# Half-angle features in place of the octant form, spread over thirteen steps

## The chip, the cores and the metric

One Trainium2 chip, one of its cores. The metric is the device time of the whole kernel in microseconds; lower is better. Engines: TensorE (PE, weight loads PEld), VectorE (DVE), ScalarE (ACT), GpSimd (POOL), SyncE (SP).

## The reference

Three chunked self-attention layers (8 heads, chunks of 64, followed by a residual and a layer norm) and one neighbour layer, on 32 batches of 128 x 1024. The change lies in the neighbour layer. It takes for each of 1024 points of three coordinates the 30 nearest, and from each difference three features:

```python
idx = _knn(x_loc, k)
rel = pts[bidx, idx] - pts[:, :, None, :]
xr, yr, zr = (rel[..., 0], rel[..., 1], rel[..., 2])
sxy2 = xr * xr + yr * yr
r2 = sxy2 + zr * zr
rho = jnp.sqrt(jnp.maximum(r2, TINY))
sxy = jnp.sqrt(jnp.maximum(sxy2, TINY))
theta = jnp.arctan2(jnp.where(deg_r, 0.0, zr), jnp.where(deg_r, 1.0, sxy))
phi = jnp.arctan2(jnp.where(deg_p, 0.0, yr), jnp.where(deg_p, 1.0, xr))
feat = jnp.concatenate([sph, sph - jnp.mean(sph, axis=-1, keepdims=True)], axis=-1)
h = lrelu(_bn(feat @ W1.T, g1, b1))
...
att = jax.nn.softmax(h[..., 0], axis=-1)
agg = jnp.einsum('bnkc,bnk->bnc', xk, att)
```

Here deg_r and deg_p are r2 < TINY and sxy2 < TINY, and sph is the three features.

## The kernel before

Three stages stand behind one another. attention_and_neighbours does the attention layers, the neighbour search and the features; batch_norms reads the features back and makes the attention weights of the neighbours; neighbour_sum adds them up. A barrier ends each stage. The change touches the first stage and one line of the second.

The first stage walks through 32 batches in steps. A batch has 24 steps (3 layers x 8 pairs of chunks); a loop body holds two batches, 48 steps. All engines run the same step function, each with its own part, in order, and semaphores tie them together. In each step TensorE makes the scores of one pair (SC, two buffers), VectorE takes their row_max (L1065), ScalarE makes the exponentials (L724, eight with a read of the sum), VectorE inverts the sum one step later (row_rec, L1073), GpSimd multiplies (L845), TensorE transposes three steps later, ScalarE copies that out (prob_t, L731), and so on. The scores of step s need the exponentials of step s - 2. Between these stand the projections and their copies (q_t, k_t, v_b), and VectorE's search for the 32 nearest (MAX8, FIND_INDEX8, MATCH_REPLACE8).

Work on a finished batch lags behind: the function lagging(i, s, at) gives the batch whose work with lag `at` belongs into step s, counted from the first step of that batch's attention plus 24. The lag numbers are the order written out by hand. In lags 8 to 33 the neighbours' coordinates are fetched tile by tile (hot L1104 on VectorE, fetch on TensorE, picked L750 on ScalarE, select on GpSimd, every third step). Then come the features of 256 x 128 differences, as tiles of 128 x 256 per quantity:

- lag 34 GpSimd: apart, the difference (L941). Lag 35 ScalarE: sqr, its squares (L761).
- lag 36 GpSimd: r2, two sums (L947, L949); r2m, its maximum with TINY (L952); good, its test against TINY (L953).
- lag 38 ScalarE: root (L767). Lag 39 and 40 GpSimd: degen (L959), yy (L960), xx (L962, L966, L970).
- lag 41 ScalarE: Abs of yy and xx (L771, L772). Lag 42 ScalarE: signs (L777, L778, L780); VectorE: big, the larger (L1109), and its reciprocal (L1112).
- lag 43 VectorE: the smaller (L1115) and a flag (L1116). Lag 44 ScalarE: turn, quarter (L784, L785), arctangent (L790); GpSimd: ratio (L975).
- lag 45 to 47 GpSimd: angle times turn, plus quarter, the half turn, the sign (L980 to L996). Lag 47 SyncE: three stores.

Root and arctangent need other tables of ScalarE than the exponential: a table load stands before each, and one before the next exponential. After the last batch, TAIL = 48 further steps finish the lagging work.

## Time and profile before

| | |
|---|---|
| median of 3 runs | 6427.92 us (6425.65 to 6432.02) |
| profiled execution | 6420.67 us, span 6418.8 us |
| first stage | to about 4741 us of the span |
| granted TensorE clock, mean | 0.919 |
| touched instructions before | GpSimd 15, ScalarE 10, VectorE 4 for each batch |

Times are microseconds from the start of the span. Busy times of neighbouring instructions on one engine overlap slightly, so start to start is the better measure of what one costs its engine. In brackets stands the idle time of the engine before an instruction and what ended it.

### The profile page before, as it was taken

To read this page: it belongs to the slowest core of one execution; us is meant where nothing else is said; L and a number is where in the kernel's file an instruction comes from. 1 tells how busy PE (TensorE), PEld (TensorE's weight loads), DVE (VectorE), ACT (ScalarE), POOL (GpSimd) and SP (SyncE) were. 2 spreads that over 40 slices of the span, in tenths; PEclk is the share of its full clock that TensorE was granted. 3 is DMA by queue.
4 is the path that set the end of the run, shared out by engine and by line. 5 is a ranking of instruction groups with operands and counts; after the bars stand their busy time and mean duration, and the time that the engine had idled before them with its cause. 6 is when DMAs were issued, how large, how long until landed. Compare 5 with 4: busy or idle time off the path is not lost. (4 is left out here: it accounts for less than half of the span.)

```text
span 6418.8 us, 227467 instructions
## 1 busy us (share of the span) xinstructions
PE 5554.2 (87%) x82516; PEld 3410.8 (53%) x82516; DVE 5771.8 (90%) x8140; ACT 4559.4 (71%) x17241; POOL 3506.7 (55%) x3471
## 2 busy tenths in 40 slices
PE   7988888889888888888888888888759949999999
PEld 3555555555555555455555555455423337777776
DVE  7999999999999999999999999999946687777776
ACT  7888888888888888888888888888713633333333
POOL 3466666666666666666666666666640023333332
PEclk9999999989999999999999999999869979999999
DMA  2333333333333333233333333333340023333332
GB/s 44 94 105 93 98 96 95 90 95 104 100 103 96 97 96 96 88 95 98 105 101 99 96 96 97 89 95 101 97 122 0 0 59 84 86 92 91 86 90 75
DMA packets 651349, 568.72 MB, mean 89 GB/s; under 512 B 553072, under 2 KB 574832, under 8 KB 616208
## 3 DMA queue, kind: packets, MB, share of 16 engines
q1 hardware_dynamic: 613264, 284.51, 18.9%
q10 hardware_dynamic: 36864, 268.45, 11.6%
q8 instruction: 702, 11.50, 0.7%
q14 instruction: 519, 4.25, 0.2%
HBM read 384.76 MB, written 67.24 MB: 70 GB/s over the span
## 5 line engine op out<-in xcount | busy, mean ns | idle before, releaser
L724 ACT ACTIVATE prob<-SC,row_max 128x64 f32<-128x64 f32 x6144 | 1841.8, 337 | 423.5 <-DVE row_max L1065 415.5
L845 POOL TENSOR_TENSOR prob<-prob,row_rec 128x512 f32<-128x512 f32 x768 | 800.6, 1042 | 1413.3 <-DVE row_rec L1073 1405.0
L724 ACT ACTIVATION_READ_ACCUMULATOR prob<-SC,row_max 128x1 f32 x6144 | 1393.1, 229 | 0.0
L1057 DVE FIND_INDEX8 nbr<-top,dist 128x8 uint16<-128x1024 f32 x1024 | 1236.2, 1220 | 0.0
L1050 DVE MAX8 top<-dist 128x8 f32<-128x1024 f32 x1024 | 1192.1, 1206 | 1.6
L1052 DVE MATCH_REPLACE8 dist<-top,dist 128x1024 f32<-128x1024 f32 x768 | 925.4, 1210 | 0.0
L588 PE MATMUL SC<-k_bd,q_t 128*64 128x256 f32 x6144 | 906.3, 419 | 0.0
L609 PE MATMUL PT<-ident,prob 128*128 128x128 f32 x3072 | 503.9, 289 | 463.6 <-ACT prob_t L731 462.8
L609 PEld LDWEIGHTS PT<-ident,prob 128*128 128x128 f32 x3072 | 374.5, 148 | 941.6 <-issue 909.9
L1721 ACT ACTIVATE dense<-DM 128x512 f32<-128x512 f32 x512 | 305.6, 597 | 745.6 <-PE DM L1680 745.0
L1829 DVE TENSOR_TENSOR d_oh_a<-lo,iota_a 128x4096 bf16<-128x4096 bf16 x256 | 583.8, 2291 | 237.8 <-PE DM L1680 237.3
L560 PEld LDWEIGHTS G<-table,low_all 128*128 128x128 bf16 x24576 | 672.3, 97 | 189.3 <-issue 112.2
L560 PE MATMUL G<-table,low_all 128*128 128x24 bf16 x24576 | 708.6, 175 | 58.5 <-DVE low_all L1104 33.1
L1680 PEld LDWEIGHTS DM<-placed,d_oh_a 128*128 128x128 bf16 x24576 | 646.5, 96 | 110.8 <-issue 77.7
L1680 PE MATMUL DM<-placed,d_oh_a 128*128 128x32 bf16 x24576 | 652.0, 177 | 30.8 <-DMA placed<-compact 22.5
L1065 DVE TENSOR_REDUCE row_max<-SC 128x8 f32<-128x512 f32 x768 | 522.0, 680 | 96.5 <-PE SC L588 96.2
L588 PEld LDWEIGHTS SC<-k_bd,q_t 128*64 128x64 f32 x6144 | 396.0, 144 | 321.3 <-issue 222.3
L602 PE MATMUL PD<-ctx 128*128 128x512 f32 x1024 | 544.3, 613 | 0.0
L731 ACT ACTIVATE prob_t<-PT 128x512 f32<-128x512 f32 x768 | 498.4, 649 | 0.6 <-PE PT L609 0.6
L1658 PE MATMUL AG<-dense,x_t 128*128 128x512 f32 x1024 | 474.4, 606 | 1.1 <-issue 0.7
L717 ACT ACTIVATE dist<-PD,xcol 128x512 f32<-128x512 f32 x512 | 369.6, 722 | 135.3 <-PE PD L602 118.9
L538 PE MATMUL PJ<-ctx,w_in 128*128 128x512 f32 x768 | 439.0, 654 | 0.1
(195 smaller groups left out, 9805.5 us busy)
## 6 DMA issues: line engine op xcount, KB each, us to landing
low_all<-low_scratch ACTq DMA_DIRECT2D x256, 1024.0 KB, 5.1
k_bd<-k_t SPq DMA_DIRECT2D x3072, 16.0 KB, 1.9
placed<-compact SPq DMA_DIRECT2D x256, 192.0 KB, 3.9
ctx<-in_ctx SPq DMA_DIRECT2D x32, 512.0 KB, 4.0
mask<-in_mask SPq DMA_DIRECT2D x32, 512.0 KB, 6.7
xb<-in_x SPq DMA_DIRECT2D x32, 512.0 KB, 3.4
x_scratch<-xb SPq DMA_DIRECT2D x32, 512.0 KB, 4.7
y_scratch<-y_b SPq DMA_DIRECT2D x32, 512.0 KB, 4.7
```

The costliest lines, as they stand in the source:

```text
L560: last = pe.matmul(G[:, g * 24:(g + 1) * 24], hot[:, t % 2, col:col + 128], table[:, v % BPB, part, :], start=(part == 0), stop=(part == 2))
L588: last = pe.matmul(bank[64 * ch:64 * ch + 64, cols], q_t[:, w % 2, here], k_bd[:, s // 2 % KEY_BUFS, s % 2 * 2 + ch, cols], start=False, s ...
L602: pe.matmul(PD[:, :], ctx[:, u, t * 128:(t + 1) * 128], ctx[:, u, h * HALF:(h + 1) * HALF], start=False, stop=True).then_inc(pd_ready, 1)
L609: last = pe.transpose(PT[:, m * 128:(m + 1) * 128], prob[:, r % 4, m * 128:(m + 1) * 128], ident[:, :])
L724: last = act.activation(prob[:, s % 4, g * CHUNK:(g + 1) * CHUNK], SC[:, s % 2, g * CHUNK:(g + 1) * CHUNK], ACT.Exp, bias=row_max[:, s % 2 ...
L845: pool.tensor_tensor(pr, pr, row_rec[:, r % 2, :].unsqueeze(2).to_broadcast([128, 8, CHUNK]), ALU.mult).then_inc(normed, 1)
L1050: dve.max(best, row).then_inc(top_step, 1)
L1052: dve.match_replace(row, best, row, NEG_BIG).then_inc(top_step, 1)
L1057: last = dve.max_index(nbr[:, uu % BPB, t, k * 8:(k + 1) * 8], best, row)
L1065: dve.tensor_reduce(row_max[:, s % 2, :], SC[:, s % 2, :].rearrange("p (h k) -> p h k", h=8), AX.X, ALU.max, negate=True).then_inc(maxed, 1)
L1680: last = pe.matmul(DM[:, x % DM_BANKS, (g % 16) * 32:(g % 16 + 1) * 32].rearrange("p (q m) -> p q m", q=4), oh_a[:, t % 2, g, :], placed[: ...
L1829: dve.tensor_tensor(oh_a[:, t % 2, :, :].rearrange("p g (a two) -> p g a two", two=2), lo2[:, u, t, :, :].unsqueeze(2).to_broadcast(wide), ...
```

## The change

The arctangents are taken of half the angle: tan(a / 2) = y / (hypotenuse + |x|). That needs no comparison of |x| and |y|, no smaller and larger, no quarter turn. The root is taken of three quantities instead of two (r2m gets a third column, made by a third sum on GpSimd), `sides` holds them and |across|. `base` is the sum of two neighbouring sides on GpSimd, inverted on VectorE at lag 43; `ratio` is legs times that. Abs and signs are of half the width and all stand at lag 41 on ScalarE. `turn` on GpSimd at lag 45 gives the half turn of the second angle, and two half-width operations at lag 46 end the work. The stores stay at lag 47. The two tensor_scalar of lag 36 get a second operation, times 1.0. The missing factor 2 goes into two columns of the next stage's weights.

```diff
@@ -47,14 +47,15 @@
 LINKS = 7
-TABLE_LINKS, SELECT_LINKS, TURN_LINKS = 4, 3, 4
+TABLE_LINKS, SELECT_LINKS, R2_LINKS = 4, 3, 3
 
 HOT_AT, FETCH_AT, SELECT_AT = 8, 10, 12
-APART_AT, R2_AT, YX_AT, ABS_AT, RATIO_AT, ANGLE_AT, TURN_AT, SPH_AT = 34, 36, 39, 41, 42, 44, 46, 47
-TAIL = SPH_AT + 1
+APART_AT, SQUARE_REL_AT, R2_AT, ROOT_AT, LEGS_AT, ACROSS_AT, BASE_AT, INVERSE_AT = 34, 35, 36, 38, 39, 41, 42, 43
+RATIO_AT, ANGLE_AT, TURN_AT, SPH_AT, SPH_OUT_AT = 44, 44, 45, 46, 47
+TAIL = SPH_OUT_AT + 1
 GROUPS = 32
@@ -222,16 +223,14 @@
         r2 = sb("r2", [128, 2, NF])
-        r2m = sb("r2m", [128, 2, NF])
-        root = sb("root", [128, 2, NF])
+        r2m = sb("r2m", [128, 3, NF])
+        sides = sb("sides", [128, 4, NF])
         good = sb("good", [128, 2, NF])
-        degen = sb("degen", [128, 2, NF])
-        yy = sb("yy", [128, 2, NF])
-        xx = sb("xx", [128, 2, NF])
-        big, ratio = sqr[:, 0:2, :], apart[:, 0:2, :]
+        legs = sb("legs", [128, 2, NF])
+        signs = sb("signs", [128, 2, NF])
         angle = sb("angle", [128, 2, NF])
-        hot, ay, ax, flag, sph = low_all, r2, r2m, r2, angle
-        turn, quarter, down_sign, left_sign, left_half = good, degen, yy, xx[:, 1, :], xx[:, 0, :]
+        hot, ratio, base = low_all, apart[:, 0:2, :], sqr[:, 0:2, :]
+        across, turn, left_half = r2[:, 0, :], r2[:, 1, :], good[:, 0, :]
 
...
@@ -496,15 +495,14 @@
                             sp.dma_start(own[32 * q:32 * q + 32, c, :, :], mine[row, q:q + 1].broadcast_to([32, NT, GROUPS])).then_inc(own_in, 16)
-                v = lagging(i, s, SPH_AT)
+                v = lagging(i, s, SPH_OUT_AT)
                 if v is not None:
                     b = i * BPB + v
-                    sp.wait_ge(root_ready, START + b + 1)
                     sp.wait_ge(sph_ready, START + b + 1)
                     alone(sp)
-                    sp.dma_start(dram["sph"][0][b], root[:, 0, :]).then_inc(sph_out, 16)
+                    sp.dma_start(dram["sph"][0][b], sides[:, 0, :]).then_inc(sph_out, 16)
                     for c in range(2):
-                        sp.dma_start(dram["sph"][1 + c][b], sph[:, c, :]).then_inc(sph_out, 16)
+                        sp.dma_start(dram["sph"][1 + c][b], angle[:, c, :]).then_inc(sph_out, 16)
 
@@ -755,34 +753,26 @@
                     load_low(i, at[0], at[1] + 2)
-                v = lagging(i, s, APART_AT + 1)
+                v = lagging(i, s, SQUARE_REL_AT)
                 if v is not None:
                     act.activation(sqr[:, :, :], apart[:, :, :], ACT.Square).then_inc(sqr_ready, 1)
-                v = lagging(i, s, R2_AT + 2)
+                v = lagging(i, s, ROOT_AT)
                 if v is not None:
                     b = i * BPB + v
-                    act.wait_ge(good_ready, START + b + 1)
+                    act.wait_ge(r2_ready, START + b + 1)
                     act.wait_ge(sph_out, START + b * 48)
-                    act.activation(root[:, :, :], r2m[:, :, :], ACT.Sqrt).then_inc(root_ready, 1)
-                v = lagging(i, s, ABS_AT)
-                if v is not None:
-                    act.wait_ge(yx_ready, START + i * BPB + v + 1)
-                    act.activation(ay[:, :, :], yy[:, :, :], ACT.Abs)
-                    act.activation(ax[:, :, :], xx[:, :, :], ACT.Abs).then_inc(abs_ready, 1)
-                v = lagging(i, s, ABS_AT + 1)
+                    act.activation(sides[:, 0:3, :], r2m[:, :, :], ACT.Sqrt).then_inc(sides_ready, 1)
+                v = lagging(i, s, ACROSS_AT)
                 if v is not None:
                     b = i * BPB + v
-                    act.wait_ge(abs_ready, START + b + 1)
-                    act.activation(down_sign[:, :, :], yy[:, :, :], ACT.Sign, scale=SIGN_SCALE, bias=turns[:, 0:1])
-                    act.activation(left_sign[:, :], xx[:, 1, :], ACT.Sign, scale=SIGN_SCALE, bias=turns[:, 0:1]).then_inc(signs_ready, 1)
-                    act.wait_ge(signs_ready, START + b + 1)
-                    act.activation(left_half[:, :], left_sign[:, :], ACT.Identity, scale=-float(np.pi / 2), bias=turns[:, 1:2])
-                v = lagging(i, s, RATIO_AT + 2)
-                if v is not None:
-                    act.wait_ge(least_ready, START + i * BPB + v + 1)
-                    act.activation(turn[:, :, :], flag[:, :, :], ACT.Identity, scale=-2.0, bias=1.0)
-                    act.activation(quarter[:, :, :], flag[:, :, :], ACT.Identity, scale=float(np.pi / 2))
+                    act.wait_ge(legs_ready, START + b + 1)
+                    act.wait_ge(sph_out, START + b * 48)
+                    act.activation(sides[:, 3, :], across, ACT.Abs).then_inc(across_ready, 1)
+                    act.activation(signs[:, 0, :], across, ACT.Sign, scale=SIGN_SCALE, bias=turns[:, 0:1]).then_inc(sign_step, 1)
+                    act.activation(signs[:, 1, :], legs[:, 1, :], ACT.Sign, scale=SIGN_SCALE, bias=turns[:, 0:1])
+                    act.wait_ge(sign_step, START + b + 1)
+                    act.activation(left_half, signs[:, 0, :], ACT.Identity, scale=-float(np.pi / 4), bias=turns[:, 1:2]).then_inc(signs_ready, 1)
                 v = lagging(i, s, ANGLE_AT)
@@ -843,6 +833,12 @@
                     pool.tensor_tensor(pr, pr, row_rec[:, r % 2, :].unsqueeze(2).to_broadcast([128, 8, CHUNK]), ALU.mult).then_inc(normed, 1)
+                v = lagging(i, s, BASE_AT)
+                if v is not None:
+                    b = i * BPB + v
+                    pool.wait_ge(sides_ready, START + b + 1)
+                    pool.wait_ge(across_ready, START + b + 1)
+                    pool.tensor_tensor(base[:, :, :], sides[:, 1:3, :], sides[:, 2:4, :], ALU.add).then_inc(base_ready, 1)
                 part = s % BSTEPS - SPLIT_AT
@@ -945,55 +941,40 @@
                     pool.tensor_tensor(r2[:, 1, :], sqr[:, 0, :], sqr[:, 2, :], ALU.add).then_inc(r2_step, 1)
-                    pool.wait_ge(r2_step, START + b + 1)
-                    pool.tensor_tensor(r2[:, 0, :], r2[:, 1, :], sqr[:, 1, :], ALU.add).then_inc(r2_ready, 1)
-                    pool.wait_ge(r2_ready, START + b + 1)
+                    pool.wait_ge(r2_step, START + b * R2_LINKS + 1)
+                    pool.tensor_tensor(r2[:, 0, :], r2[:, 1, :], sqr[:, 1, :], ALU.add).then_inc(r2_step, 1)
+                    pool.wait_ge(r2_step, START + b * R2_LINKS + 2)
                     alone(pool)
-                    pool.tensor_scalar(r2m[:, :, :], r2[:, :, :], TINY, None, ALU.max)
-                    pool.tensor_scalar(good[:, :, :], r2[:, :, :], TINY, None, ALU.is_ge).then_inc(good_ready, 1)
-                v = lagging(i, s, YX_AT)
+                    pool.tensor_scalar(r2m[:, 0:3:2, :], r2[:, :, :], TINY, 1.0, ALU.max, ALU.mult).then_inc(r2_step, 1)
+                    pool.tensor_scalar(good[:, :, :], r2[:, :, :], TINY, 1.0, ALU.is_ge, ALU.mult).then_inc(good_ready, 1)
+                    pool.wait_ge(r2_step, START + b * R2_LINKS + 3)
+                    pool.tensor_tensor(r2m[:, 1, :], r2m[:, 2, :], sqr[:, 1, :], ALU.add).then_inc(r2_ready, 1)
+                v = lagging(i, s, LEGS_AT)
                 if v is not None:
                     pool.wait_ge(good_ready, START + b + 1)
+                    pool.wait_ge(r2_ready, START + b + 1)
                     alone(pool)
-                    pool.tensor_scalar(degen[:, :, :], good[:, :, :], -1.0, 1.0, ALU.mult, ALU.add).then_inc(degen_ready, 1)
-                    pool.tensor_tensor(yy[:, :, :], apart[:, 1:3, :], good[:, :, :], ALU.mult)
-                    pool.wait_ge(root_ready, START + b + 1)
-                    pool.tensor_tensor(xx[:, 0, :], root[:, 1, :], good[:, 0, :], ALU.mult)
-                v = lagging(i, s, YX_AT + 1)
+                    pool.tensor_tensor(across, apart[:, 0, :], good[:, 1, :], ALU.mult)
+                    pool.tensor_tensor(legs[:, :, :], apart[:, 1:3, :], good[:, :, :], ALU.mult).then_inc(legs_ready, 1)
+                v = lagging(i, s, TURN_AT)
                 if v is not None:
                     b = i * BPB + v
-                    pool.tensor_tensor(xx[:, 1, :], apart[:, 0, :], good[:, 1, :], ALU.mult).then_inc(yx_step, 1)
-                    pool.wait_ge(yx_step, START + b + 1)
-                    pool.wait_ge(degen_ready, START + b + 1)
-                    alone(pool)
-                    pool.tensor_tensor(xx[:, :, :], xx[:, :, :], degen[:, :, :], ALU.add).then_inc(yx_ready, 1)
-                v = lagging(i, s, ANGLE_AT)
+                    pool.wait_ge(signs_ready, START + b + 1)
+                    pool.tensor_tensor(turn, left_half, signs[:, 1, :], ALU.mult).then_inc(turn_ready, 1)
+                v = lagging(i, s, RATIO_AT)
                 if v is not None:
                     b = i * BPB + v
-                    pool.wait_ge(least_ready, START + b + 1)
-                    pool.tensor_tensor(ratio[:, :, :], ratio[:, :, :], big[:, :, :], ALU.mult).then_inc(ratio_ready, 1)
-                v = lagging(i, s, ANGLE_AT + 1)
+                    pool.wait_ge(inverse_ready, START + b + 1)
+                    pool.tensor_tensor(ratio[:, :, :], legs[:, :, :], base[:, :, :], ALU.mult).then_inc(ratio_ready, 1)
+                v = lagging(i, s, SPH_AT)
                 if v is not None:
                     pool.wait_ge(angle_ready, START + b + 1)
-                    pool.tensor_tensor(angle[:, :, :], angle[:, :, :], turn[:, :, :], ALU.mult).then_inc(turn_step, 1)
-                v = lagging(i, s, TURN_AT)
-                if v is not None:
-                    b = i * BPB + v
-                    pool.wait_ge(turn_step, START + b * TURN_LINKS + 1)
-                    alone(pool)
-                    pool.tensor_tensor(angle[:, :, :], angle[:, :, :], quarter[:, :, :], ALU.add).then_inc(turn_step, 1)
-                    pool.wait_ge(turn_step, START + b * TURN_LINKS + 2)
-                    pool.tensor_tensor(angle[:, 1, :], angle[:, 1, :], left_sign[:, :], ALU.mult).then_inc(turn_step, 1)
-                    pool.wait_ge(turn_step, START + b * TURN_LINKS + 3)
-                    pool.tensor_tensor(angle[:, 1, :], angle[:, 1, :], left_half[:, :], ALU.add).then_inc(turn_step, 1)
-                v = lagging(i, s, SPH_AT)
-                if v is not None:
-                    b = i * BPB + v
-                    pool.wait_ge(turn_step, START + b * TURN_LINKS + 4)
-                    alone(pool)
-                    pool.tensor_tensor(sph[:, :, :], angle[:, :, :], down_sign[:, :, :], ALU.mult).then_inc(sph_ready, 1)
+                    pool.wait_ge(turn_ready, START + b + 1)
+                    pool.tensor_tensor(angle[:, 1, :], angle[:, 1, :], signs[:, 0, :], ALU.mult).then_inc(flip_step, 1)
+                    pool.wait_ge(flip_step, START + b + 1)
+                    pool.tensor_tensor(angle[:, 1, :], angle[:, 1, :], turn, ALU.add).then_inc(sph_ready, 1)
 
@@ -1102,18 +1083,11 @@
                     dve.tensor_scalar(hot[:, t % 2, :], low_all[:, t % 2, :], iota_p[:, 0:1], None, ALU.is_equal).then_inc(hot_ready, 1)
-                v = lagging(i, s, RATIO_AT)
+                v = lagging(i, s, INVERSE_AT)
                 if v is not None:
                     b = i * BPB + v
-                    dve.wait_ge(abs_ready, START + b + 1)
-                    dve.tensor_tensor(big[:, :, :], ax[:, :, :], ay[:, :, :], ALU.max).then_inc(big_step, 1)
-                    dve.wait_ge(big_step, START + b + 1)
-                    alone(dve)
-                    dve.reciprocal(big[:, :, :], big[:, :, :])
-                v = lagging(i, s, RATIO_AT + 1)
-                if v is not None:
-                    dve.tensor_tensor(ratio[:, :, :], ax[:, :, :], ay[:, :, :], ALU.min)
-                    dve.tensor_tensor(flag[:, :, :], ay[:, :, :], ax[:, :, :], ALU.is_gt).then_inc(least_ready, 1)
+                    dve.wait_ge(base_ready, START + b + 1)
+                    dve.reciprocal(base[:, :, :], base[:, :, :]).then_inc(inverse_ready, 1)
 
@@ -1392,6 +1367,7 @@
             link(dve.scalar_tensor_tensor(v1[:, :, :], w1s[:, :].unsqueeze(2).to_broadcast([128, 6, 3]), -1.0 / 3.0, v1[:, :, :], ALU.mult, ALU.add))
+            link(dve.tensor_scalar(v1[:, :, 1:3], v1[:, :, 1:3], HALF_ANGLES, None, ALU.mult))
 
@@ -1941,7 +1917,7 @@
     out["pow_half"] = np.full((128, 1), -0.5, np.float32)
-    out["turns"] = np.tile(np.array([SIGN_TIE, np.pi / 2], np.float32), (128, 1))
+    out["turns"] = np.tile(np.array([SIGN_TIE, np.pi / 4], np.float32), (128, 1))
     out["iota8"] = high_bits(np.tile(np.arange(8, dtype=np.float32)[None, :], (128, 1)))
```

## Rows read from the trace of the kernel before

**Rows 1.** The page, part 1: busy us (share of the span) and instructions
```profile
PE 5554.2 (87%) x82516; PEld 3410.8 (53%) x82516; DVE 5771.8 (90%) x8140; ACT 4559.4 (71%) x17241; POOL 3506.7 (55%) x3471
```

**Rows 2.** Windows from:to: length, busy us of PE PEld DVE ACT POOL, PEclk, DMA
```profile
1000.00:4000.00 3000.00, 2627.53 (x36246) 1563.56 (x36243) 2926.67 (x4505) 2587.56 (x10644) 1975.67 (x2056) 0.92 0.34 97
...
4620.00:4741.00 121.00, 36.47 (x1116) 32.46 (x1116) 48.53 (x49) 32.30 (x56) 89.41 (x89) 0.53 0.32 111
```

**Rows 3.** Waits: who waited for whom, us in total, times, longest us
```profile
DVE row_max L1065 <- PE SC L588: 96.2, 59, 14.0
```

**Rows 4.** Timeline of VectorE, lags 42 and 43: start us, us, instruction
```profile
2132.29 1.46 DVE L1109 TENSOR_TENSOR sqr<-r2m,r 128x512 f32<-128x512 f32 x1
...
2133.90 3.35 DVE L1112 RECIPROCAL sqr<-sqr 128x512 f32<-128x512 f32 x1
...
2141.36 0.68 DVE L1115 TENSOR_TENSOR apart<-r2m,r 128x512 f32<-128x512 f32 x1
...
2142.56 0.69 DVE L1065 TENSOR_REDUCE row_max<-SC 128x8 f32<-128x512 f32 x1
```

**Rows 5.** Timeline of ScalarE, lag 44
```profile
2146.71 0.70 ACT L784 ACTIVATE good<-r 128x512 f32<-128x512 f32 x1
...
2147.93 1.28 ACT L790 ACT_TABLE_LOAD   x1
```

**Rows 6.** Timeline of TensorE, lags 44 and 46, with idle time before in brackets
```profile
2140.95 1.09 PE L609 MATMUL PT<-ident,prob 128*128 128x128 f32 x4 [5.47 <-ACT prob_t L731]
...
2156.01 0.76 PE L609 MATMUL PT<-ident,prob 128*128 128x128 f32 x4 [2.27 <-ACT prob_t L731]
```

**Rows 7.** Window of TensorE's scores for lag 47
```profile
2158.00:2162.00 4.00, 4.00 (x57) 2.77 (x56) 2.07 (x6) 3.38 (x19) 3.77 (x6) 0.50 0.09 37
```

**Rows 8.** Timeline of VectorE: first, middle and last of 30 waits at lag 47
```profile
422.71 0.69 DVE L1065 TENSOR_REDUCE row_max<-SC 128x8 f32<-128x512 f32 x1 [1.44 <-PE SC L588]
...
2161.23 0.69 DVE L1065 TENSOR_REDUCE row_max<-SC 128x8 f32<-128x512 f32 x1 [1.93 <-PE SC L588]
...
4615.11 0.69 DVE L1065 TENSOR_REDUCE row_max<-SC 128x8 f32<-128x512 f32 x1 [1.81 <-PE SC L588]
```

**Rows 9.** Groups of ScalarE, root and Square: busy us, mean ns, idle before
```profile
L767 ACT ACTIVATE root<-r2m 128x512 f32<-128x512 f32 x32 | 20.2, 631 | 7.6 <-POOL good L953 7.3
...
L761 ACT ACTIVATE sqr<-apart 128x768 f32<-128x768 f32 x32 | 29.0, 906 | 6.0 <-POOL apart L941 6.0
```

**Rows 10.** Timeline of TensorE at lag 40 and of VectorE into lag 41
```profile
2110.31 0.37 PE L583 MATMUL SC<-mask_row,two_chunks 64*128 64x512 bf16 x1 [1.90 <-ACT v_b L677]
...
2118.74 1.21 DVE L1052 MATCH_REPLACE8 dist<-top,dist 128x1024 f32<-128x1024 f32 x1
...
2119.95 0.69 DVE L1065 TENSOR_REDUCE row_max<-SC 128x8 f32<-128x512 f32 x1
```

**Rows 11.** Groups of GpSimd: busy us, mean ns of one, idle before
```profile
L952 POOL TENSOR_SCALAR r2m<-r 128x512 f32<-128x512 f32 x32 | 49.2, 1537 | 6.2 <-POOL r L949 6.2
...
L959 POOL TENSOR_SCALAR degen<-good 128x512 f32<-128x512 f32 x32 | 19.8, 619 | 0.3 <-POOL good L953 0.2
...
L970 POOL TENSOR_TENSOR xx<-xx,degen 128x512 f32<-128x512 f32 x32 | 40.8, 1274 | 6.5 <-POOL xx L966 6.5
...
L966 POOL TENSOR_TENSOR xx<-apart,good 128x256 f32<-128x256 f32 x32 | 23.4, 732 | 0.0
```

**Rows 12.** Timeline of GpSimd, last batch, first and last instruction of its features
```profile
4710.24 1.80 POOL L941 TENSOR_TENSOR apart<-rel,own 128x768 f32<-128x768 f32 x1
...
4736.73 1.26 POOL L996 TENSOR_TENSOR angle<-angle,yy 128x512 f32<-128x512 f32 x1 [0.18 <-POOL angle L990]
```

**Rows 13.** Timeline of ScalarE, root of the last batch but one
```profile
4665.04 0.63 ACT L767 ACTIVATE root<-r2m 128x512 f32<-128x512 f32 x1 [3.84 <-POOL good L953]
```

**Rows 14.** Timeline of ScalarE and GpSimd at lag 42
```profile
2127.69 0.31 ACT L724 ACTIVATE prob<-SC,row_max 128x64 f32<-128x64 f32 x1 [0.35 <-DVE row_max L1065]
...
2128.15 1.03 POOL L845 TENSOR_TENSOR prob<-prob,row_rec 128x512 f32<-128x512 f32 x1
```

17 lines of the change are left out of this document (9 added, 8 removed).

## Prediction

> **What bounds the kernel now.** I read the busy line of the page first: VectorE 90%, TensorE 87%, ScalarE 71%, GpSimd 55% [rows 1]. An average over stages doesn't name a bound, so the windows came next [rows 2]. From 1000 to 4000 us VectorE is busy 2926.67 of 3000 us (97.6%), ScalarE 86%, GpSimd 66%. From 4620 to 4741 us no engine is full, GpSimd leads with 89.41 of 121 us, and the granted clock of TensorE is 0.53, near its lower level of 1.2 GHz. So the first stage has a steady part that VectorE paces, and a tail that is a chain. The waits then say where VectorE's missing 2.4% goes: into row_max waiting for TensorE's scores, 96.2 us in all [rows 3].
>
> The touched work runs once for each of 32 batches: 30 times in the steady part, twice in the tail. I name steps by lag: "lag 42" is RATIO_AT of before.
>
> **VectorE, steady part.** Removed are max (L1109), min (L1115) and is_gt (L1116). The reciprocal stays and moves from lag 42 to 43. Busy times overlap the next instruction, so I take start to start [rows 4]: L1109 to L1112 2133.90 - 2132.29 = 1.61 us; L1115 to the row_max of the next step 2142.56 - 2141.36 = 1.20 us. Together 2.81 us a batch, all of it on the engine that paces and none of it waiting. L1109 is stretched (1.46 us busy, where the like-shaped min has 0.68); without that the gain would be 0.78 less. I take the record: 30 x 2.81 = 84.3 us. The moved reciprocal (3.35 us) makes lag 42 some 5.0 us shorter and lag 43 2.1 us longer. Its result goes to `ratio` on GpSimd at lag 44, which is queued behind a normalisation that needs a row_rec that VectorE issues after the reciprocal, so nobody waits longer for it. ScalarE is no limit there: it waits for row_max in both steps.
>
> **ScalarE.** Ten activations become seven. The switches to root and arctangent and back stay, so no table load is saved. What counts is lag 44, where `turn` and `quarter` stood ahead of the arctangent: 2147.93 - 2146.71 = 1.22 us [rows 5]. Queued behind it are copies, the reload of the exponential's table, the exponentials and prob_t. TensorE then waits 2.27 us for that prob_t [rows 6] and goes on at a granted clock of 0.50, 1.2 GHz [rows 7]; VectorE waits 1.93 us for the scores that follow [rows 8]. This happens at lag 47 in all 30 steady batches, first at 422.71 and last at 4615.11 us, 54.1 us in sum, 0.38 (two of them) to 2.34 us each [rows 8]. ScalarE 1.22 us earlier takes as much from 28 waits and all of two: 28 x 1.22 + 2 x 0.38 = 34.9 us. Bounds: 0 (TensorE late for a reason of its own) and 54.1 (its clock stays at 2.4 GHz). I take 34.9, because TensorE will reach that prob_t earlier than now and still idle some 2 us before it. The activations gone at lag 41 and 42 are worth nothing, since ScalarE then waits for VectorE; lag 41 itself gets four half-width operations for two full ones, some 0.5 us more, in that spare time.
>
> The root goes from 512 to 768 columns: 631 ns, against 906 for the Square of 768 [rows 9], 0.27 us more. It has no cover. TensorE waits 1.90 us at lag 40 for a v_b copy queued behind the root, and at lag 41 row_max starts 1.21 us after the operation before it, the whole busy time, without the usual overlap of 0.08 [rows 10]: this chain is just late. 30 x 0.27 = 8.2 us lost; bounds 0 and 15 (if TensorE's slow clock also lasts longer).
>
> **GpSimd.** Fifteen instructions, 15.7 us, become twelve. A two-input one takes 1274 ns for 512 columns and 732 for 256, a tensor_scalar with two operations 619 (L959) [rows 11]. New sum: seven half-width ones 5.1, three full ones (legs, base, ratio) 3.85, r2m and good 1.24: 10.2 us. The 5.5 us less are worth nothing in the steady part, where GpSimd mostly waits for row_rec. `base` at lag 42 now stands ahead of the row split and the selection of a tile, for which ScalarE's copy of the next tile waits. By adding up the queue the selection ends about when ScalarE comes: nothing, at most 1 us a batch if ScalarE has no spare time there. Sharing of memory access with VectorE shifts both ways; I keep 10 us either way.
>
> The neutral second operation (max, then times 1) is to bring r2m and good from 1537 ns down to 619 [rows 11]. L952 has one operation, L959 two; but L959 is mult and add, so the rows leave open whether the count or the kind decides. I take the count. The price is 1.8 us for each of two batches in the tail, nothing in the steady part.
> The Trainium skill (GPSIMD Engine Reference, "3.1 Elementwise — side-by-side cycle accounting") has a body of up to two operations bound by its port at 1.03 cycles an element, which makes the two forms equal and the edit worthless. L952 against L959 speaks against the rule here; by it the sum would be the third rival's.
>
> **The tail.** The last batch's features run from `apart` at 4710.24 to the end of L996 at 4738.0 us, 27.8 us with nothing beside them [rows 12]. Out of that chain go, at the durations of rows 4 and 11: degen 0.62, one half-width product 0.72, xx plus degen and its fence 1.46, max and its fence 0.84, min and is_gt 1.20, the tensor_scalar saving 1.75, angle times turn and plus quarter 2.78, the last product 1.44, the narrower Abs 0.3, and 1.15 of table load, since a root here starts right at the end of a wait for GpSimd, its load done within it [rows 13]. Into it: third column 0.73, base 1.27. 12.26 - 2.00 = 10.3 us. Before that, features of the last batch but one hold up the last one's tiles; I give this GpSimd's 5.5 us and 1.5 us of waits for Abs and min: 7 us, bounds 0 and 15. Tail: 17.3 us. Doubling two weight columns in the next stage costs some 0.2 us once.
>
> **Sum.** 84.3 + 34.9 - 8.2 + 17.3 - 0.2 = 128.1 us. The profiled execution took 6420.67 us (span 6418.8), which gives 6292.6; it lies 7.25 us under the median of 6427.92. Comparisons go by medians, so the forecast is 6427.92 - 128.1 = 6300 us. Nothing else changes behind 4741 us.
>
> **Rivals.** First: TensorE's clock stays up from lag 45 on and those waits vanish. For it: the idle time of 5.47 us at lag 44 [rows 6] nearly goes. Against: it still idles for prob_t. 19.2 us more: 6281 us.
> Second: the saving is given back. If the scores come at a pace set by ScalarE and TensorE, VectorE arrives earlier and waits. For it: the late row_max at lag 41 and 47. Against: before 2140.95 TensorE idles 5.47 us, so it is ahead where VectorE gains. Price: half of 84.3 and all of 34.9: 6300 + 42 + 35 = 6377 us.
> Third: the neutral operation does nothing, all else holds: 3.5 us more in the tail, 6303 us.
> Fourth, slower: GpSimd's wait for `across` at lag 42, ahead of split, selection and the next normalisation. ScalarE is through lag 41 before 2127.69, when its 0.35 us wait ends, so `across` is there by 2127.8; GpSimd gets to the wait at 2128.15 + 1.03 = 2129.2 [rows 14]. 1.4 us are spare; past that each microsecond delays tile copy and exponentials. The sum turns at 128 / 30 = 4.3 us more, 5.7 us late; at 6.5 us late it is 6300 + 30 x 5.1 = 6453 us. Nothing in the record has ScalarE that late.
>
> **Chances.** Forecast 0.57, rivals 0.15, 0.13, 0.11 and 0.02, the remaining 0.02 within 0.2%, which is 13 us and about what a measurement of this kernel tells from no change. Faster 0.95, same 0.02, slower 0.03 (the fourth and a hundredth for the unseen). Range: the low end adds to the first rival a tail of 25 us and part of the some 23 us of waits outside lag 47 and the first steps: 6260. The high end has VectorE's 84.3 with 10 us of contention against it and a tail of 7: 6347.
>
> **What would show it.** L1109, L1115, L1116 gone and L1112 still 3.35 us; the pitch of the batches down from (4615.11 - 422.71) / 29 = 144.6 us to about 140.9; row_max's wait at lag 47 near 0.65 us instead of 1.8; at lag 41 a new wait of 0.2 to 0.3; r2m and good at 0.62 us (third rival: 1.5); the stage ending near 4613 instead of 4741 us. The forecast is wrong if row_max's waits don't shrink, if ScalarE or GpSimd waits for base, across or the selection, or if the reciprocal runs longer in its new place.

## The result: 6319.5 us, and the profile after

The kernel with the change took 6319.46 us (median of 4 runs, 6316.55 to 6323.72), beside it the kernel before 6429.97 us (4 runs, 6425.65 to 6432.29). The ratio is 0.9829, with a 95% interval of 0.9812 to 0.9846: faster by 110.5 us, where 128.1 were forecast. The profiled execution has a span of 6314.8 us, against 6418.8.

First the page of the kernel after, part 1, which answers to [rows 1]:

```profile
PE 5517.6 (87%) x82516; PEld 3384.3 (54%) x82516; DVE 5699.2 (90%) x8045; ACT 4499.4 (71%) x17145; POOL 3397.5 (54%) x3375
```

VectorE's busy time fell by 72.6 us, not by 84.3. The windows of the same kernel (length, busy us of PE, PEld, DVE, ACT, POOL, granted clock, DMA share, GB/s):

```profile
1000.00:4000.00 3000.00, 2655.17 (x36940) 1576.22 (x36937) 2940.94 (x4536) 2603.24 (x10807) 1938.98 (x2030) 0.94 0.35 99
4513.00:4634.00 121.00, 46.60 (x1281) 39.15 (x1281) 53.62 (x62) 39.03 (x103) 92.82 (x96) 0.55 0.34 120
```

VectorE is now busy 98.0% of the steady part instead of 97.6% [rows 2]: it is the bound as before, and even more so. The last 121 us of the stage are still a chain of GpSimd at a low granted clock. Where the time went is read from the groups (line, engine, operation, tiles, count | busy us, mean ns of one | idle before):

```profile
L1046 DVE TENSOR_REDUCE row_max<-SC 128x8 f32<-128x512 f32 x768 | 518.6, 675 | 73.7 <-PE SC L586 73.3
L1085 DVE TENSOR_SCALAR low_all<-low_all,iota_p 128x4096 bf16<-128x4096 bf16 x256 | 364.1, 1422 | 34.5 <-DMA low_all<-low_scratch 34.5
...
L1090 DVE RECIPROCAL sqr<-sqr 128x512 f32<-128x512 f32 x32 | 106.8, 3338 | 22.4 <-POOL sqr L841 22.4
...
L835 POOL TENSOR_TENSOR prob<-prob,row_rec 128x512 f32<-128x512 f32 x768 | 830.2, 1082 | 1433.5 <-DVE row_rec L1054 1403.5 <-issue 30.0
...
L948 POOL TENSOR_SCALAR r2m<-r 128x512 f32<-128x512 f32 x32 | 62.0, 1936 | 6.2 <-POOL r L945 6.2
L949 POOL TENSOR_SCALAR good<-r 128x512 f32<-128x512 f32 x32 | 61.8, 1932 | 2.5
```

Four things stand there. The wait of row_max for scores went from 96.2 [rows 3] to 73.3 us. `r2m` takes 1936 ns, not 619 and not 1537 [rows 11]. L1085, a line the change doesn't touch, got longer: this compare (it turns a tile's low indices into a one-hot matrix, 256 of them) took 347.1 us before, 1356 ns each, and takes 364.1 now, 1422 ns. And the multiplication on `prob` on GpSimd, 1042 ns before, takes 1082. The compares also explain the first number: the three removed instructions took 2.79 us a batch on the mean from start to start, 89.3 us in 32 batches, and 89.3 less 17.0 is 72.3.

The timeline of VectorE of the kernel after, first and last wait at lag 47, which answer to [rows 8]:

```profile
418.69 0.69 DVE L1046 TENSOR_REDUCE row_max<-SC 128x8 f32<-128x512 f32 x1 [1.45 <-PE SC L586]
...
4520.94 0.69 DVE L1046 TENSOR_REDUCE row_max<-SC 128x8 f32<-128x512 f32 x1 [1.26 <-PE SC L586]
```

(4520.94 - 418.69) / 29 = 141.46 us a batch, against 144.56: 3.10 us less, 3.70 forecast. All 30 waits are still there, 33.8 us in sum instead of 54.1. From the last of them to the end of the stage, which is the minus_half memset at 4634.12 us (4741.40 before), 113.2 us pass instead of 126.3: the tail gives 13.1 us.

From here on "pitch" is the mean distance of the reciprocals of batches 1 to 30, L1090 or its like (before 144.57, after 141.48, so 3.10 less before rounding), and "waits" are those of row_max for scores behind the first of them (before 76.5 us, after 54.2).

### The profile page after: what moved, and what is told of

Read it like the earlier page. It is cut to its first block and busy times, and to the rows that moved or that the text cites. A ratio compares the mean times of both kernels' runs of the same rounds, so it can differ in the third digit from the quotient of the medians.

```text
span 6314.8 us, 227176 instructions
## 1 busy us (share of the span) xinstructions
PE 5517.6 (87%) x82516; PEld 3384.3 (54%) x82516; DVE 5699.2 (90%) x8045; ACT 4499.4 (71%) x17145; POOL 3397.5 (54%) x3375
## 5 line engine op out<-in xcount | busy, mean ns | idle before, releaser
L835 POOL TENSOR_TENSOR prob<-prob,row_rec 128x512 f32<-128x512 f32 x768 | 830.2, 1082 | 1433.5 <-DVE row_rec L1054 1403.5
L607 PEld LDWEIGHTS PT<-ident,prob 128*128 128x128 f32 x3072 | 361.7, 145 | 833.8 <-issue 815.6
L607 PE MATMUL PT<-ident,prob 128*128 128x128 f32 x3072 | 490.9, 284 | 351.0 <-ACT prob_t L729 350.3
L1046 DVE TENSOR_REDUCE row_max<-SC 128x8 f32<-128x512 f32 x768 | 518.6, 675 | 73.7 <-PE SC L586 73.3
```

The costliest lines, as they stand in the source:

```text
L607: last = pe.transpose(PT[:, m * 128:(m + 1) * 128], prob[:, r % 4, m * 128:(m + 1) * 128], ident[:, :])
L835: pool.tensor_tensor(pr, pr, row_rec[:, r % 2, :].unsqueeze(2).to_broadcast([128, 8, CHUNK]), ALU.mult).then_inc(normed, 1)
```

## The experiments

Three theories were tried, each against the others. A: ScalarE's load at lag 44 sets the wait at lag 47. B: the kind of operation, not its count, sets what GpSimd's tensor_scalar costs. C, formed from the compare above: GpSimd's timing decides how long VectorE's compares take. All ratios are against the kernel before, measured beside each run; its median was 6431.34 us beside the first four, 6430.24 beside the next four and 6426.98 beside the last two. The kernel of the change did not run beside them, so a difference to its 6319.46 us can be off by some 4 us from that alone. Medians are of four executions, except ten for the neutral operations on the kernel before and two for the narrow root.

### Neutral second operations taken away

```diff
-pool.tensor_scalar(r2m[:, 0:3:2, :], r2[:, :, :], TINY, 1.0, ALU.max, ALU.mult).then_inc(r2_step, 1)
-pool.tensor_scalar(good[:, :, :], r2[:, :, :], TINY, 1.0, ALU.is_ge, ALU.mult).then_inc(good_ready, 1)
+pool.tensor_scalar(r2m[:, 0:3:2, :], r2[:, :, :], TINY, None, ALU.max).then_inc(r2_step, 1)
+pool.tensor_scalar(good[:, :, :], r2[:, :, :], TINY, None, ALU.is_ge).then_inc(good_ready, 1)
```

> The changed kernel, the two tensor_scalar of lag 36 with one operation again. Theory A (the second operation lengthens r2m and good from 1.5 to 1.94 us, GpSimd gets late, its normalisation at lag 38 falls on VectorE's compare and stretches it from 1.28 to 1.83 us): both at 1.50, the compare of lag 38 back to 1.28, pitch of the batches 141.5 down to 141.0 to 141.2 us, time 6319 less 10 to 17 us. Rival B (GpSimd's length is covered in the steady part, as the prediction had it): same pitch, only the tail 1 to 2 us shorter, 6317 us. Rival C (the second operation pays): slower by 1.8 us in each of two tail batches.

Measured: 6316.82 us (6310.49 to 6318.49), ratio 0.982 (0.9802 to 0.9837), pitch 141.53. `r2m` and `good` take 1508 and 1497 ns. The second operation costs 0.43 us each time and buys nothing, and in the steady part it costs no time. From the last lag-47 wait (4524.32) to the end of the stage (4634.64) it is 110.3 us, 2.9 less than with the second operations.

Rival B holds for the time, and theory A failed at its main point: the compare at lag 38 stayed long in every batch from 400 to 4500 us, 1.76 us on the mean instead of the expected 1.28. From the timeline of this run, lag 38:

```profile
1503.10 1.05 POOL L835 TENSOR_TENSOR prob<-prob,row_rec 128x512 f32<-128x512 f32 x1
...
1503.47 1.77 DVE L1085 TENSOR_SCALAR low_all<-low_all,iota_p 128x4096 bf16<-128x4096 bf16 x1
```

With the shorter `r2m` and `good` the addition on `y_b` is done in time, but the multiplication on `prob` behind it now starts 0.37 us ahead of the compare. In the same batch of the kernel before it starts 1.06 us ahead (1526.23, compare at 1527.29) and ends just in time. The difference, 0.69 us, is about the third column's addition, 0.73 us, which stands in GpSimd's chain here and not before. So that addition is enough to make the compare late. It was not taken out by itself.

### VectorE's three operations put back

They work on tiles that are there (max into `r2m` at lag 42, min into `apart` and is_gt into a spare tile at lag 43); what they compute is used by nobody.

```diff
+                v = lagging(i, s, BASE_AT)
+                if v is not None:
+                    dve.wait_ge(base_ready, START + i * BPB + v + 1)
+                    dve.tensor_tensor(r2m[:, 0:2, :], legs[:, :, :], legs[:, :, :], ALU.max)
 ...
+                    dve.tensor_tensor(apart[:, 0:2, :], legs[:, :, :], legs[:, :, :], ALU.min)
+                    dve.tensor_tensor(spare[:, :, :], legs[:, :, :], legs[:, :, :], ALU.is_gt)
-                    dve.wait_ge(base_ready, START + b + 1)
                     dve.reciprocal(base[:, :, :], base[:, :, :]).then_inc(inverse_ready, 1)
```

> The changed kernel with three two-input VectorE operations of the removed length put back (one at lag 42, two at lag 43), results unused. Theory A (VectorE paces, each is paid in full): pitch up by 0.60 + 0.60 for two and 0.6 to 1.6 for the first, 1.8 to 2.8 us a batch, time 6319 + 58 to 90 us, the waits at lag 47 unchanged at 0.4 to 1.45 us. Rival B (the saving was partly given back in waits): pitch up by less than 1.4 us, 45 us in all, and the waits at lag 47 get shorter.

Measured: 6399.49 us (6392.86 to 6401.77), ratio 0.9953 (0.9935 to 0.997), pitch 143.73, 2.25 more than after. Its row of the waits (total us, times, longest):

```profile
DVE row_max L1047 <- PE SC L587: 57.5, 48, 13.6
```

The three put back take 2.90 us a batch here, start to start (0.59, 0.87 and 1.44 by the trace; those of the kernel before took 1.59, 0.60 and 0.60). The pitch shows 2.25 of it. The rest is mostly paid out of waits (73.3 after, in the count of this row): behind the first reciprocal they fall from 54.2 to 38.7 us, 0.53 a batch. 2.25 + 0.53 = 2.78, against the forecast's 2.81. So the pitch and time are theory A's, and the shorter waits at lag 47 are rival B's.

The waits at lag 47 alone are 14.3 us here, in 16 of 30 batches. Against the 54.1 of before, 39.8 are gone without VectorE's gain, where the forecast had 34.9; the reciprocal stands one step later than before in this run too, so not all of it need be ScalarE's. With VectorE's gain on top, 33.8 us are left: 19.5 of the 39.8 come back as waits.

### ScalarE's two activations put back at lag 44

```diff
+                    act.activation(spare[:, :, :], legs[:, :, :], ACT.Identity, scale=-2.0, bias=1.0)
+                    act.activation(r2m[:, 0:2, :], legs[:, :, :], ACT.Identity, scale=float(np.pi / 2))
                     act.activation(angle[:, :, :], ratio[:, :, :], ACT.Arctan).then_inc(angle_ready, 1)
```

> The changed kernel with two 512-column activations put back ahead of the arctangent at lag 44, results unused. Theory A (the wait of row_max at lag 47 hangs on ScalarE's chain): the waits at lag 47 rise from a mean of 1.13 to between 1.8 and 2.3 us, pitch up by 0.7 to 1.2 us, time 6319 + 20 to 36 us. Rival B (that wait is set by TensorE or its clock alone): no change of pitch, 6319 to 6323 us.

Measured: 6340.23 us (6337.77 to 6356.56), ratio 0.9858 (0.984 to 0.9876), 20.8 us more than the kernel of the change, at the low end of theory A. The profile is of the longest of the four executions, 16 us above the median, so its pitch of 142.75 (1.28 more than after) and its waits show more than the median lost. The row of its waits:

```profile
DVE row_max L1049 <- PE SC L587: 101.0, 60, 13.3
```

27.7 us of waits more than after. 13.9 of them are at lag 47, where the mean is 1.59 us (47.7 us over 30 batches), less than the 1.8 to 2.3 expected; 9.5 come one step later. Rival B (no change) is out: the four executions lie 14 us and more above all four of the kernel of the change. ScalarE's queue at lag 44 does lengthen these waits (A), but not only at lag 47.

### Reciprocal, ratio and arctangent one step earlier

The other side of the same question: if that step is too full, take the arctangent out of it.

```diff
-... BASE_AT, INVERSE_AT = ... 42, 43
-RATIO_AT, ANGLE_AT, TURN_AT, SPH_AT, SPH_OUT_AT = 44, 44, 45, 46, 47
+... BASE_AT, INVERSE_AT = ... 42, 42
+RATIO_AT, ANGLE_AT, TURN_AT, SPH_AT, SPH_OUT_AT = 43, 43, 45, 46, 47
```

> The changed kernel with reciprocal, ratio and arctangent one lag earlier (42, 43, 43). Theory A (two table loads at lag 44 stand just ahead of the steps in which ScalarE also copies v, so they make the wait at lag 47; at lag 43 ScalarE is idle 2 us): waits at lag 47 gone or under 0.4 us, pitch 141.5 down to 140.3 to 140.8, 6319 less 20 to 34 us. Rival B (the loads make the same wait one step earlier, at lag 46): pitch unchanged within 0.2 us. Rival C (row_max comes later behind the reciprocal at lag 42 and ScalarE loses the slack): slower by up to 20 us.

Measured: 6276.64 us (6273.56 to 6277.83), ratio 0.976 (0.9742 to 0.9777), pitch 140.09: 43 us faster than the kernel of the change, more than the 20 to 34 of theory A. Its waits, its windows beside and behind the arctangent (2084.73 us), and then the same stretch of the kernel after:

```profile
DVE row_max L1046 <- PE SC L586: 36.2, 27, 14.1
```

```profile
2084.00:2086.00 2.00, 2.00 (x11) 0.78 (x12) 2.00 (x5) 1.97 (x4) 1.23 (x2) 0.50 0.03 8
2086.00:2088.00 2.00, 2.00 (x52) 1.56 (x51) 2.00 (x5) 1.99 (x6) 0.84 (x1) 0.68 0.05 8
2090.00:2100.00 10.00, 9.36 (x175) 6.47 (x173) 10.00 (x18) 9.96 (x44) 8.26 (x7) 1.00 0.40 129
```

```profile
2104.01 1.28 ACT L780 ACT_TABLE_LOAD   x1
2105.30 0.63 ACT L780 ACTIVATE angle<-apart 128x512 f32<-128x512 f32 x1
2106.41 0.68 ACT L708 ACTIVATE y_b<-PJ,b_out 128x512 f32<-128x512 f32 x1
...
2107.14 1.15 PE L543 MATMUL PJ<-w_in,ctx 128*64 128x64 f32 x32 [1.32 <-ACT y_b L708]
...
2112.10 0.95 PE L607 MATMUL PT<-ident,prob 128*128 128x128 f32 x4 [2.62 <-ACT prob_t L729]
...
2117.51 0.69 DVE L1046 TENSOR_REDUCE row_max<-SC 128x8 f32<-128x512 f32 x1 [1.31 <-PE SC L586]
```

In the kernel after, table load and arctangent stand in the step that has ScalarE's copy of `y_b` too. TensorE waits 1.32 us for that copy, then 2.62 for prob_t (2.27 before [rows 6]), goes on at a granted clock of 0.50 from 2114 to 2118 us, and VectorE waits 1.31 us. One step earlier the arctangent meets no such copy, and no wait at lag 47 is left in any batch. The granted clock falls here too, but earlier: it is 0.50 from 2084 to 2086 us and 0.68 in the two behind, after TensorE had idled 2.19 us for a prob_t (to 2082.92). VectorE is busy all through these windows. In the ten microseconds that hold the scores for lag 47 (2097.82 to 2099.22) it is 1.00. The mean over the whole program is the same in both, 0.936 and 0.935. So the forecast's first rival (the clock stays up from lag 45 on, those waits vanish) is reached by moving the low stretch to where nobody waits, and the change alone doesn't do that.

### The neutral second operations alone, on the kernel before

```diff
-pool.tensor_scalar(r2m[:, :, :], r2[:, :, :], TINY, None, ALU.max)
-pool.tensor_scalar(good[:, :, :], r2[:, :, :], TINY, None, ALU.is_ge).then_inc(good_ready, 1)
+pool.tensor_scalar(r2m[:, :, :], r2[:, :, :], TINY, 1.0, ALU.max, ALU.mult)
+pool.tensor_scalar(good[:, :, :], r2[:, :, :], TINY, 1.0, ALU.is_ge, ALU.mult).then_inc(good_ready, 1)
```

> The kernel before with one part of the change alone: the two neutral second operations of GpSimd (max with mult, is_ge with mult) at the step of R2_AT. Theory C (GpSimd's chain there decides when its additions on y_b and the multiplication on prob run, and a compare of VectorE that runs beside a GpSimd instruction is stretched): the chain gets some 0.9 us longer, the multiplication on prob, which ended at 1380.56 us, 0.02 us before the compare at lag 38 began, now runs beside it, and that compare goes from 1.27 to about 1.8 us; pitch of the batches 144.57 to about 145.1, time 10 to 16 us more, compares' mean about 1.42 us. Rival (the second operation costs nothing, as taking it from the changed kernel did): pitch within 0.1 us of 144.57, compares' mean 1.356 us, time within 3 us of before. A second rival, that of the forecast (max and is_ge fall to 619 ns with a second operation): both stay under 0.7 us; the changed kernel's 1.93 us already speaks against it.

Measured: 6429.63 us (6425.28 to 6436.74), ratio 1.0001 (0.9991 to 1.001), pitch 144.80; `r2m` and `good` at 1932 and 1931 ns, the compares at 1362. No time was lost, so theory C as I had put it was wrong: the chain did get 0.9 us longer, the multiplication on `prob` did come to lie beside the compare at lag 38, and the compare there stayed at 1.27 us in 22 of 28 batches (in the other six it took about 2.1). The timeline of this kernel shows why, in two batches:

```profile
1530.12 3.18 POOL L845 TENSOR_TENSOR prob<-prob,row_rec 128x512 f32<-128x512 f32 x2
1530.13 1.28 DVE L1104 TENSOR_SCALAR low_all<-low_all,iota_p 128x4096 bf16<-128x4096 bf16 x1
...
1820.32 1.04 POOL L845 TENSOR_TENSOR prob<-prob,row_rec 128x512 f32<-128x512 f32 x1
1820.34 2.10 DVE L1104 TENSOR_SCALAR low_all<-low_all,iota_p 128x4096 bf16<-128x4096 bf16 x1
```

The same two instructions, almost the same start. In the first the compare goes through and the two multiplications in the group take 3.18 us in all; in the second GpSimd goes through in 1.04 us and the compare takes 2.10. One of the two waits for the other to end, and the order of their starts decides which. In the six batches with a long compare the multiplication starts 0.01 or 0.02 us ahead. At 0.01 us ahead both outcomes are seen (the first of these two batches, and the compare at 2980.65 us with 2.11 us), and at a later start the compare always went through.

### `good` two steps later

```diff
-                    pool.tensor_scalar(good[:, :, :], r2[:, :, :], TINY, 1.0, ALU.is_ge, ALU.mult).then_inc(good_ready, 1)
 ...
+                v = lagging(i, s, R2_AT + 2)
+                if v is not None:
+                    pool.wait_ge(r2_step, START + (i * BPB + v) * R2_LINKS + 3)
+                    alone(pool)
+                    pool.tensor_scalar(good[:, :, :], r2[:, :, :], TINY, 1.0, ALU.is_ge, ALU.mult).then_inc(good_ready, 1)
```

> The changed kernel with `good` (is_ge) taken out of GpSimd's chain at R2_AT and issued two steps later, ahead of its first user; same work, same operations. Theory C: GpSimd's chain is 2.0 us shorter there, its y_b addition and the multiplication on prob end before VectorE's compare at lag 38 begins, and that compare goes back from 1.83 to 1.27 us; pitch 141.48 to about 140.9 to 141.0, time about 15 us less (6300 to 6306). Rival (the stretch is due to ScalarE's table load and root beside it, or to the order of VectorE's own instructions): the compare stays at 1.83 us, pitch and time stay within 0.1 us and 3 us of the changed kernel. Third case: the compare shortens but VectorE waits as much more for the scores at lag 47 (33.8 us to about 45): time unchanged.

Measured: 6313.72 us (6311.28 to 6317.75), ratio 0.9824 (0.9807 to 0.984), pitch 141.29. Less than half of it came. From the timeline of the kernel after, lags 38 and 41, and then of this one, lag 38:

```profile
1356.59 1.27 POOL L860 TENSOR_TENSOR y_b<-y_b,xb 128x512 f32<-128x512 f32 x1
...
1357.11 1.84 DVE L1085 TENSOR_SCALAR low_all<-low_all,iota_p 128x4096 bf16<-128x4096 bf16 x1
...
1374.88 1.27 POOL L860 TENSOR_TENSOR y_b<-y_b,xb 128x512 f32<-128x512 f32 x1
1375.25 1.99 DVE L1085 TENSOR_SCALAR low_all<-low_all,iota_p 128x4096 bf16<-128x4096 bf16 x1
```

```profile
1355.54 1.04 POOL L835 TENSOR_TENSOR prob<-prob,row_rec 128x512 f32<-128x512 f32 x1
1356.66 2.15 POOL L955 TENSOR_SCALAR good<-r 128x512 f32<-128x512 f32 x1
1356.85 1.51 DVE L1089 TENSOR_SCALAR low_all<-low_all,iota_p 128x4096 bf16<-128x4096 bf16 x1
```

The addition on `y_b` and the multiplication are out of the way now, and in their place `good` itself runs beside the compare. Both are stretched, the compare from 1.27 to 1.51 us and `good` from 1.93 to 2.15, but neither waits for the other's end.

### The root 512 columns wide again

```diff
-act.activation(sides[:, 0:3, :], r2m[:, :, :], ACT.Sqrt).then_inc(sides_ready, 1)
+act.activation(sides[:, 0:2, :], r2m[:, 0:2, :], ACT.Sqrt).then_inc(sides_ready, 1)
 ...
-pool.tensor_tensor(base[:, :, :], sides[:, 1:3, :], sides[:, 2:4, :], ALU.add).then_inc(base_ready, 1)
+pool.tensor_tensor(base[:, :, :], sides[:, 0:2, :], sides[:, 1:4:2, :], ALU.add).then_inc(base_ready, 1)
```

> The changed kernel with ScalarE's root 512 columns wide again instead of 768 (a third of the roots is left out, and the sums take two of the tiles that are there, so the angles are not the reference's). Forecast's term (root wider, no cover): the root goes from 844 to about 631 ns, and 0.2 us a batch come back: pitch 141.48 to about 141.27, 6 us less. Rival (the wider root is covered like the rest of ScalarE's work at lag 38): pitch within 0.05 us of 141.48.

Measured: 6318.94 us (6318.57 to 6319.31), ratio 0.983 (0.981 to 0.985), pitch 141.485 with the root at 630 ns, 141.477 with 844. The wider root costs nothing.

### Both moves together

> The changed kernel with the reciprocal, ratio and arctangent one step earlier (the move that brought the pitch to 140.09 us and the time to 6276.6) and `good` two steps later. Theory C and additive parts: compare at lag 38 at 1.27 us, pitch about 139.5 to 139.6, time about 6260 to 6264. Rival (VectorE's gain is given back as waits for scores now that it is the bound nearly everywhere): pitch 140.0 to 140.1, time 6275, and the waits for scores rise from 18 us by some 15. Rival (compare stays stretched): as the last, without more waits.

Measured: 6271.3 us (6267.56 to 6272.12), ratio 0.9754 (0.9738 to 0.977), pitch 139.88, waits 17.4 us. Between the expectations: 5 us faster than the earlier arctangent alone, with the compare at lag 38 at 1.53 us and the one at lag 41 still at 1.96 on the mean.

### `good` in the step of its first user

```diff
-                    pool.tensor_scalar(good[:, :, :], r2[:, :, :], TINY, 1.0, ALU.is_ge, ALU.mult).then_inc(good_ready, 1)
 ...
-                    pool.wait_ge(good_ready, START + b + 1)
                     pool.wait_ge(r2_ready, START + b + 1)
                     alone(pool)
+                    pool.tensor_scalar(good[:, :, :], r2[:, :, :], TINY, 1.0, ALU.is_ge, ALU.mult).then_inc(good_ready, 1)
+                    pool.wait_ge(good_ready, START + b + 1)
+                    alone(pool)
```

> The changed kernel with `good` (is_ge) issued three steps later, in the step of LEGS_AT just ahead of its first user; same work. The rows of the run with `good` two steps later suggest a rule: VectorE's compare and a GpSimd instruction on two tiles don't run at once, the one that starts second waits for the other, and a GpSimd tensor_scalar beside the compare stretches both by 0.2 us. By it GpSimd is idle from 1356.6 us of that batch to the next row_rec, the compare at lag 38 (which starts at 1356.85) takes 1.27 us, `good` 1.93 us, no multiplication on prob is over 1.07 us; pitch about 140.9 to 141.1, time 6303 to 6311. Rival (the stretch belongs to the compare at that place, whatever GpSimd does): 1.5 us or more.

Measured: 6279.33 us (6275.47 to 6288.53), ratio 0.9767 (0.9751 to 0.9783), pitch 140.43: 40 us faster than the kernel of the change, for one instruction moved. That is more than expected, and the timeline (lags 38 and 41) and the group of the compares tell why:

```profile
1349.47 1.04 POOL L835 TENSOR_TENSOR prob<-prob,row_rec 128x512 f32<-128x512 f32 x1
1350.75 1.27 DVE L1086 TENSOR_SCALAR low_all<-low_all,iota_p 128x4096 bf16<-128x4096 bf16 x1
...
1368.64 1.27 DVE L1086 TENSOR_SCALAR low_all<-low_all,iota_p 128x4096 bf16<-128x4096 bf16 x1
1368.68 2.37 POOL L860 TENSOR_TENSOR y_b<-y_b,xb 128x512 f32<-128x512 f32 x1
```

```profile
L1086 DVE TENSOR_SCALAR low_all<-low_all,iota_p 128x4096 bf16<-128x4096 bf16 x256 | 328.8, 1284 | 34.1 <-DMA low_all<-low_scratch 34.0
```

At lag 38 nothing of GpSimd lies beside the compare. At lag 41 the compare now starts 0.04 us ahead of GpSimd's addition where it was 0.37 us behind: it takes 1.27 us instead of 1.99, and it is GpSimd that waits (2.37 us for 1.27), in time that it has. It is GpSimd that got later. Counted from the row_max of lag 40 the compare starts at 5.32 us in both kernels (from 1369.93 after, from 1363.32 here), the addition at 4.95 after and 5.36 here, because `good` now stands in GpSimd's queue at lag 39. So it is in 26 of 29 batches. This part of the gain was not expected; it is luck of the new place. The compares take 35.3 us less than after (364.1, 328.8), 1.22 over 29 pitches; the pitch fell by 1.04. The profile is of the longest of the four executions, 9 us above the median.

### All moves together

> The same with the reciprocal, ratio and arctangent one step earlier as well. By the same rule the compare at lag 38 takes 1.27 us; pitch 139.5 to 139.8 if VectorE's 0.24 us a batch against the kernel with both moves stays a gain, time 6262 to 6271. Rival (given back as waits for scores): pitch 139.9, waits 18 to 25 us, time 6271. `good` now stands in GpSimd's step at lag 39 and the sums of `base` at lag 42 are unaffected; were legs late for abs at lag 41, ScalarE would show a wait for them.

Measured: 6248.45 us (6247.31 to 6249.63), ratio 0.9722 (0.9706 to 0.9738), pitch 139.13: below the range expected, again because the compare at lag 41 came free too (at both lags 1.27 us in every batch). The pitch falls by 2.35 us against the kernel after, and 1.39 + 1.04 = 2.43 was the sum of the two moves alone. By the medians they add up less well: 42.8 and 40.1 us alone, 71.0 together. Why some 12 us are missing stays open. ScalarE's wait for `legs`, the sign named in the expectation, did come, in the last two batches alone: 8.5 us in sum, 3.5 in the kernel after. This version is 71 us faster than the kernel of the change and 179 us faster than the one before.

## Why the prediction was right, and where its sum was off

The forecast time, 6300 us, is 19 us low, inside the range; the working is right in direction in each large term and wrong in smaller ones, some of which cancel. A batch, by the forecast and as measured:

| Term, us a batch | forecast | measured | from |
|---|---|---|---|
| VectorE's three instructions | -2.81 | -2.78 | put back: pitch 2.25, waits 0.53 |
| waits for scores | -1.16 | -0.77 | 76.5 to 54.2 us, over 29 pitches |
| wider root | +0.27 | 0.00 | root narrowed |
| VectorE's compares | 0 | +0.59 | 347.1 to 364.1 us, over 29 pitches |
| sum | -3.70 | -2.96 | pitch of the traces: -3.10 |

- **VectorE.** The 84.3 us held. L1109, L1115 and L1116 are gone, the reciprocal takes 3.34 us.
- **ScalarE at lag 44.** The cause held, and without VectorE's gain 39.8 us of these waits are gone, near the 34.9. What failed is adding it to VectorE's 84.3 as if the two were independent. With 2.81 us less work a batch VectorE meets the same scores sooner and waits again for 19.5 us at lag 47. This is the second rival, whose price (half of all that VectorE wins, and all of the 34.9) was far too high, but which was not nothing. The wait at lag 47, forecast near 0.65 us, is 1.13 us on the mean of 30.
- **The first rival.** Before, the granted clock was low twice a batch: 0.50 from 2140 to 2146 us, behind the 5.47 us of idle time at lag 44, and 0.50 again from 2158 to 2162. After the change the first stretch is gone (1.00 from 2096 to 2106 us) and the second is there (0.50 from 2114 to 2118). So what was said for the rival came, and what was said against it, the wait for prob_t, kept the second stretch and its waits.
- **The root.** "It has no cover" was wrong. The step looked at had row_max 1.21 us behind the operation before it, all of that operation's busy time, and I took 0.08 us of missing overlap for a chain that is just late. After the change that row_max follows at 1.12 us (2079.68 behind 2078.56), although the root is 0.21 us longer: no wait at lag 41. The sum took 8.2 us off the gain for it, and that hid part of the other misses.
- **GpSimd.** "The 5.5 us less are worth nothing in the steady part", and contention was kept only as 10 us of range. GpSimd's time is indeed worth nothing, but its timing isn't. `r2m` and `good` at 1.93 us and the third column's addition make the chain of lag 36 longer, not shorter, and push the addition on `y_b` onto the compare at lag 38: in the batches from 400 to 4500 us (28 before, 29 after) the mean there goes from 1.27 to 1.84 us, and at lag 41 from 1.81 to 1.96. The third column's addition is enough for that at lag 38 (1.76 us with `r2m` and `good` at 1.5). This is the largest piece of the miss of 0.60 us a batch: 0.59 here, 0.39 of waits and 0.03 of VectorE's instructions, against 0.27 of the root and 0.14 of rest the other way. That the total came as near as it did is partly luck.
- **The neutral operation.** I took the count of operations, from L959 (mult and add, 619 ns), and it is the kind: max and is_ge stay slow. Not even the third rival holds, since they got slower by 0.43 us each.
  The Trainium skill (GPSIMD Engine Reference, "3.1 Elementwise — side-by-side cycle accounting") makes one and two operations equal in their body; the 1508 and 1936 ns measured here for max without and with a multiplication don't agree with that, nor do 1936 and 619 ns for two pairs of operations on the same shape.
- **The tail.** 13.1 us for 17.3. The last batch's chain went from 27.8 to 20.3 us, 7.5 less for 10.3 forecast, and 2.6 of the missing 2.8 are `r2m` and `good` (1.92 and 1.93 us instead of 0.62 each); that leaves 5.6 for the batch before, where 7 were forecast. The run without the second operations gets 2.9 us back here.
- **The rest.** The stage ends at 4634.12 us, 107.3 earlier, the span is 104.0 shorter: some 3 us are lost behind the stage. That was not looked into; the medians lie 110.5 apart.
- **The fourth rival** (GpSimd waits for `across`) didn't come: GpSimd waits 1.2 us in all for sides (L841), in the last two batches alone.

## What to carry to other kernels

Two savings on two engines of the same loop are not added up before asking which waits the first one turns into the second: put each back alone and read the waits. An engine that has time to spare still costs the bound one, by when it runs: look for instructions of the bound engine on untouched lines whose mean went up, and at what GpSimd runs beside them. And look at the step in which a moved operation lands, not only at its cost: the arctangent was worth 43 us one step earlier, a comparison 40 us three steps later.
